# Two-layer cross-attention transformer on one core: the next phase's input loaded tile by tile in earlier steps, a fourth query group computed ahead, fewer last pairs kept off GpSimd

## The reference

```python
# layer 0
x = x + (attn(ln1(x) @ Wq, ln2(ctx) @ Wkv) @ Wproj + bproj)     # cross attention, 77 keys
x = x + (gelu(ln3(x) @ W1 + b1) @ W2 + b2)
# layer 1
h = ln1(x);  x = x + mha(h, h, sa_wq, sa_wk, sa_wv, sa_wo)      # self attention, 512 keys
h = ln2(x);  x = x + mha(h, ctx, ca_wq, ca_wk, ca_wv, ca_wo)    # cross attention, 77 keys
return x + (gelu(ln3(x) @ mlp_w1.T + b1) @ mlp_w2.T + b2)
```

## Time and profile before

| | |
|---|---|
| median of 3 runs | 3287.32 us (3286.9 to 3288.68) |
| the profiled execution | 3286.96 us, of which the traced span is 3285.1 us |
| mean granted PE clock over the span | 0.982 |
| busy in the span | PE 3139.8, PE weight loads 2496.9, DVE 1824.0, ACT 1576.0, POOL 1313.7 us |

### The profile page before, as it was taken

The page is one execution under the profiler, slowest core; times in us unless marked ns, Lnnn a source line. Parts: engine busy times, 40 slices in busy tenths (PEclk is TensorE's granted clock), DMA queues, the critical chain, the costliest instruction groups (busy, mean ns, idle before and its releaser), DMA issues.

```text
span 3285.1 us, 41887 instructions
## 1 busy us (share of the span) xinstructions
PE 3139.8 (96%) x14480; PEld 2496.9 (76%) x14480; DVE 1824.0 (56%) x2854; ACT 1576.0 (48%) x2984; POOL 1313.7 (40%) x1357
## 2 busy tenths in 40 slices
PE   6599999999999998999999999879999999999999
PEld 5478878888888876777777777557887788888887
DVE  4588884323233236887887788868888432222221
ACT  2366663322222234777776777646666332222222
POOL 0344551333333226666666666634455111111110
PEclk9799999999999999999999999989999999999999
DMA  4322223211111123344344434432222311111110
GB/s 144 113 68 89 84 75 128 68 52 52 46 44 43 41 103 107 103 124 121 99 115 123 123 97 113 119 86 67 89 83 75 118 56 39 39 39 39 39 39 13
DMA packets 215045, 264.33 MB, mean 80 GB/s; under 512 B 78459, under 2 KB 100579, under 8 KB 214835
## 3 DMA queue, kind: packets, MB, share of 16 engines
q1 hardware_dynamic: 214323, 260.87, 26.8%
q10 hardware_dynamic: 512, 0.79, 0.1%
HBM read 125.12 MB, written 60.42 MB: 56 GB/s over the span
## 4 chain that ended last, share of the span: by engine, by line
PE 82%; DVE 6%; issue 3%; SPq 2%; ACT 2%; DMA 2%; POOL 1%; ACTq 0%; DVEq 0%; POOLq 0%
PE L1sa_o L1083 5%; PE L1ff_f L110 4%; PE L1ff_f L112 4%; PE L1ff_f L111 4%; PE L1ff_acc L112 4%; PE L0ff_acc L110 4%; PE L1ff_acc L110 4%; PE L1ff_acc L111 4%; PE L0ff_f L110 4%; PE L0ff_acc L112 4%; PE L0ff_acc L111 3%; PE L0ff_f L112 3%; PE L0ff_f L111 3%; PE L1sa_pj L110 3%; PE L1sa_s L1038 3%; PE L1sa_pj L111 3%
## 5 line engine op out<-in xcount | busy, mean ns | idle before, releaser
L1216 DVE TENSOR_REDUCE L1sa_nmax<-L1sa_s 128x2 f32<-128x1024 f32 x256 | 310.5, 1213 | 130.1 <-PE L1sa_s L1038 129.1
L350 DVE TENSOR_TENSOR L1ff_gl<-L1ff_gf,L1ff_gh 128x512 fp32r<-128x512 f32 x128 | 95.4, 745 | 467.1 <-ACT L1ff_gh L336 467.1
L1308 POOL TENSOR_TENSOR L1sa_El<-L1sa_E,L1sa_Eh 128x1024 fp32r<-128x1024 f32 x122 | 299.2, 2453 | 128.5 <-ACT L1sa_Eh L1138 125.4
L350 DVE TENSOR_TENSOR L0ff_gl<-L0ff_gf,L0ff_gh 128x512 fp32r<-128x512 f32 x128 | 96.2, 752 | 414.8 <-ACT L0ff_gh L336 414.8
L324 ACT ACTIVATE L1ff_gf<-L1ff_f,cols 128x512 f32<-128x512 f32 x128 | 88.3, 690 | 450.8 <-PE L1ff_f L112 450.8
L324 ACT ACTIVATE L0ff_gf<-L0ff_f,cols 128x512 f32<-128x512 f32 x128 | 88.3, 690 | 431.6 <-PE L0ff_f L112 431.6
L1145 ACT ACTIVATE L1sa_E<-L1sa_st 128x1024 f32<-128x1024 f32 x256 | 258.7, 1011 | 6.0 <-PE L1sa_st L1050 5.9
L110 PE MATMUL L0ff_acc<-L0ff_Wh,L0ff_gh 128*128 128x512 f32 x512 | 200.2, 391 | 6.5 <-DVE L0ff_gl L350 6.5
L1138 ACT ACTIVATE L1sa_Eh<-L1sa_E 128x1024 fp32r<-128x1024 f32 x196 | 204.7, 1044 | 0.1
L110 PE MATMUL L0ff_f<-L0ca_hTh,L0ff_Wh 128*128 128x512 f32 x512 | 202.5, 396 | 0.0
L110 PE MATMUL L1ff_f<-L0ca_hTh,L1ff_Wh 128*128 128x512 f32 x512 | 202.1, 395 | 0.0
(11 more groups left out here) (313 smaller groups left out, 8507.6 us busy)
## 6 DMA issues: line engine op xcount, KB each, us to landing
L1sa_OLN<-L1sa_osb SPq DMA_DIRECT2D x128, 192.0 KB, 2.7
L1sa_stack_q<-L1sa_parts_q SPq DMA_DIRECT2D x128, 128.0 KB, 2.6
L1sa_stack_k<-L1sa_parts_k SPq DMA_DIRECT2D x124, 128.0 KB, 2.6
L0ff_xs<-x SPq DMA_DIRECT2D x60, 256.0 KB, 2.9
L1ff_xs<-x SPq DMA_DIRECT2D x60, 256.0 KB, 3.7
L0ca_stage<-in_x SPq DMA_DIRECT2D x32, 256.0 KB, 2.8
x<-L0ca_stage SPq DMA_DIRECT2D x32, 256.0 KB, 2.1
L0ff_stage<-in_L_w SPq DMA_DIRECT2D x32, 256.0 KB, 3.1
```

The source lines that it names most:

```text
L350: nc.vector.tensor_tensor(gl[:, j % 2, :], gf[:, j % 2, :], f32(gh[:, j % 2, :]), ALU.subtract)\
L1216: nc.vector.reduce_max(nmax[:, h % 2, 2 * (n % 2):2 * (n % 2) + 2], s_bank[:, :, :], AX.X, negate=True)\
L1308: nc.gpsimd.tensor_tensor(El[:, n % 2, :], E[:, n % 3, :], f32(Eh[:, n % 2, :]), ALU.subtract)\
```

## The change

1. `CA_AHEAD` is moved: the four loads of x go to steps 1, 2, 4, 7 (one each), the two raw weights to 13 and 16, statistics to 8 to 11, normalisation to 12 to 15, transposes to 17 to 20. x goes where wv's low part lay, the raw weights where wk's lay. `xs_second` is gone: batch 1 is loaded into `xs_first` once its transposes are made.
2. `first_keys` keeps only `place_k(0)`; `place_v(0)` comes after `last_residuals`, `place_k(1)` between the loads of batch 2 and the bias.
3. Query group 3 of the first batch joins `CA_FIRST`, in both cross attentions; its evacuation comes at s = 5.
4. `LAST_PAIRS` is 8: pairs 244 to 247 (steps 20 to 23) follow the usual pattern, with Eh of 245 and 247 and El of 244 and 246 on POOL.
5. The last head is copied into a buffer of its own, `osb_last`, and does not wait for the DMA of the head before.

```diff
-    osb = ph.sb("osb", [3 * HD, S])
+    osb, osb_last = (ph.sb(n, [3 * HD, S]) for n in ("osb", "osb_last"))
...
-                    if b == B - 1 and s == CA_AHEAD.load:
-                        ca.first_loads(sp)
+                    if b == B - 1 and s in CA_AHEAD.load:
+                        ca.first_load(sp, CA_AHEAD.load.index(s))
+                    if b == B - 1 and s in CA_AHEAD.raw:
+                        ca.first_weights(sp, CA_AHEAD.raw.index(s))
...
-                if h > 0:
+                if h == HEADS - 1:
+                    act.wait_ge(ca.x.e_hl.sem, ca.x.e_hl.at(0, KT - 1))
+                elif h > 0:
                     act.wait_ge(e_oln.sem, e_oln.no(h - 1))
...
-CA_FIRST = [("Q", 0, g) for g in range(3)]
+CA_FIRST = [("Q", 0, g) for g in range(G)]
...
-CA_AHEAD.load, CA_AHEAD.stats, CA_AHEAD.norms = 10, (12, 13, 14, 15), (17, 18, 19, 20)
-CA_AHEAD.transposes, CA_AHEAD.weights = (21, 22, 23, 24), (26, 27)
+CA_AHEAD.load, CA_AHEAD.stats, CA_AHEAD.norms = (1, 2, 4, 7), (8, 9, 10, 11), (12, 13, 14, 15)
+CA_AHEAD.raw, CA_AHEAD.weights, CA_AHEAD.transposes = (13, 16), (26, 27), (17, 18, 19, 20)
...
-LAST_PAIRS = 12
+LAST_PAIRS = 8
...
     def second_loads(sp):
-        sp.wait_ge(wt.lo.sem, wt.lo.no(WQ - 1))
+        sp.wait_ge(x.e_tr.sem, x.e_tr.at(0, KT - 1))
...
         place_k(sp, 0)
-        place_v(sp, 0)
-        place_k(sp, 1)
...
                 second_loads(sp)
                 sa.last_residuals(sp)
+                place_v(sp, 0)
...
                 load(sp, 2, t)
+            place_k(sp, 1)
             sp.dma_start(x.bias[:, :], bo_row.partition_broadcast(P)).then_inc(x.bias_in.sem, x.bias_in.unit)
...
                 if s == 1:
-                    for u in CA_FIRST[2:]:
-                        evacuate(*u)
+                    evacuate(*CA_FIRST[2])
...
+                if s == LEAD - 1:
+                    evacuate(*CA_FIRST[3])
```

More of the change, by code:

```diff
@@ L939, in line_up @@
                 sp.dma_start(OLN[HD * (h % 4):HD * (h % 4 + 1), :, :],
-                             osb[:, :]).then_inc(e_oln.sem, e_oln.unit)
+                             (osb_last if h == HEADS - 1 else osb)[:, :]).then_inc(e_oln.sem, e_oln.unit)
             ff.emitted(sp, B - 2)
@@ L1148, in o_out @@
                 act.wait_ge(e_pv.sem, e_pv.no(2 * h + 1))
-                if h > 0:
+                if h == HEADS - 1:
+                    act.wait_ge(ca.x.e_hl.sem, ca.x.e_hl.at(0, KT - 1))
+                elif h > 0:
                     act.wait_ge(e_oln.sem, e_oln.no(h - 1))
-                nc.scalar.activation(osb[:, :], o_bank[h % 2][0:KD, :], ACT.Copy).then_inc(e_ob.sem, e_ob.unit)
+                nc.scalar.activation((osb_last if h == HEADS - 1 else osb)[:, :], o_bank[h % 2][0:KD, :], ACT.Copy)\
+                    .then_inc(e_ob.sem, e_ob.unit)
             def m_copy(h):
@@ L1632 @@
             "wkl": 73728, "wvl": 81920, "wol": 90112, "parts_q": 98304, "parts_k": 102400, "V": 106496, "Eh": 122880,
-            "E": 131072, "El": 143360, "osb": 151552, "hs": 153600, "hTh": 157696, "oTh": 165888, "hTl": 174080,
-            "oTl": 182272, "rx": 190464, "OLN": 194560, "Vst": 200704, "rx_last": 200704, "onorm": 208384,
-            "nmax": 210432, "mm": 210464, "mT": 210528, "bqs": 211040, **{f"raw{i}": 65536 + 4096 * i for i in range(8)}}
+            "E": 131072, "El": 143360, "osb": 151552, "hs": 153600, "osb_last": 153600,
+            "hTh": 157696, "oTh": 165888, "hTl": 174080, "oTl": 182272, "rx": 190464, "OLN": 194560, "Vst": 200704,
+            "rx_last": 200704, "onorm": 208384, "nmax": 210432, "mm": 210464, "mT": 210528, "bqs": 211040, **{f"raw{i}": 65536 + 4096 * i for i in range(8)}}
 FF_OVER_OUTPUT = 4
@@ L1712, in cross_attention, with taken @@
     units = list(CA_FIRST)
+    def taken(kind, b, i):
+        return exists(b) and (kind, b, i) not in CA_FIRST
     for b in range(B):
         for kind, ahead, i in CA_ORDER:
-            if exists(b + ahead):
+            if taken(kind, b + ahead, i):
                 units.append((kind, b + ahead, i))
@@ L1754, in x_of @@
     def x_of(n):
-        return (xs_first, xs_second, x.xs)[min(n, 2)]
+        return xs_first if n < 2 else x.xs
     def load(sp, n, t):
@@ L1896, in lo, with first_load, first_weights @@
         ln_lo(nc, x, c).then_inc(x.e_hl.sem, x.e_hl.unit)
-    def first_loads(sp):
+    def first_load(sp, t):
+        if sa is not None and t == 0:
+            sp.wait_ge(sa.e_unit.sem, sa.values_done)
+        load(sp, 0, t)
+    def first_weights(sp, i):
         if sa is not None:
             sp.wait_ge(sa.e_unit.sem, sa.keys_done)
-        for t in range(TT):
-            load(sp, 0, t)
-        load_weights(sp, wt, 0, WQ)
+        load_weights(sp, wt, i, i + 1)
     def second_loads(sp):
-        sp.wait_ge(wt.lo.sem, wt.lo.no(WQ - 1))
+        sp.wait_ge(x.e_tr.sem, x.e_tr.at(0, KT - 1))
         for t in range(TT):
@@ L1967, in _ @@
             if sa is None:
-                first_loads(sp)
+                for t in range(TT):
+                    first_load(sp, t)
+                for i in range(WQ):
+                    first_weights(sp, i)
                 first_keys(sp)
+                place_v(sp, 0)
                 load_weights(sp, wt, WQ, WO)
@@ L2235, in _ @@
                 if s == 1:
-                    for u in CA_FIRST[2:]:
-                        finish(*u)
+                    finish(*CA_FIRST[2])
                 if s == 1 and sa is not None:
@@ L2338, in cross_attention @@
     ca.x, ca.hT, ca.TILES = x, hT, TILES
-    ca.first_loads, ca.first_keys, ca.zeros, ca.statistics, ca.rsqrt = first_loads, first_keys, zeros, statistics, rsqrt
+    ca.first_load, ca.first_weights, ca.first_keys = first_load, first_weights, first_keys
+    ca.zeros, ca.statistics, ca.rsqrt = zeros, statistics, rsqrt
     ca.normalise, ca.T, ca.whole, ca.hi, ca.lo = normalise, T, whole, hi, lo
```

9 lines of the change are left out of this document (6 added, 3 removed).

## The result

The changed kernel takes 3276.34 us (median of 7 runs, 3273.92 to 3278.64), the kernel before 3287.32 (median of 7 beside it, 3285.47 to 3289.64): ratio 0.9967, 95% interval 0.9955 to 0.9978, so 11.0 us or 0.33% faster. The profiled execution took 3278.37 us, span 3276.5. Forecast was 3273, range 3264 to 3282: the time is 3 us above the forecast and inside its range. Which terms hold is read by stage. Profiled executions of kernels that are the same up to there reach the last batch some 4 us apart (s9 is at 2073.2 us here and at 2077.3 in e1_last12), so durations between two marks are used, not ends. A mark "s16" is the start of PV's low matmul of step 16 of the last batch.

What follows compares the result with a forecast made beforehand. PE was taken as the bound, in flight 3139.8 of 3285.1 us. The terms, 3.5 + 6.3 + 0.5 + 3.9 = 14.2 us, off the profiled 3286.96 give 3272.8, at the median 3273; range 3264 to 3282.

Steps and rivals of the forecast that it cites:

- Term 1: Start of L0ca: query group 3's twelve matmuls move ahead of scores 2 into PE idle time; -3.5 us.
- The shift stays: After the start of L0ca PE is full, so the time gained there is kept.
- Term 2: PE's stall at step 14 of L1sa's last batch goes, less 0.3 remaining and 1.1 for statistics; -6.3 us.
- The loads' new places: 0: Last batch of L1sa: x loads at steps 1, 2, 4, 7 and raw weights at 13, 16 cost nothing.
- Term 3: Steps 16 to 31 of L1sa's last batch: DVE relieved, POOL becomes the bound; -0.5 us, from -6 to +7.
- in 2131.2 to 2159.7 this is won back: Later tail: pair 247's 4 to 6 us lateness is recovered, as three casts leave DVE and whole parts leave ACT.
- rival C: Tail: DVE was the whole bound and POOL keeps up; -5.9 us instead of -0.5, total 3268; chance 0.11.
- Term 4: Handover to L1ca: 4.4 from the copy, 1.3 from the clock, 1.8 lost to the later bias; -3.9 us.
- with a buffer of its own the copy follows at once: Handover: the last head's copy no longer waits for head 126's line-up DMA; gains 4.4 us.
- A: The stall moves: a load or statistic delays maxima in a PE-full step, no step-14 gain; 3279; chance 0.11.
- B: Tail: four new POOL instructions each block a DVE operation for their whole length; +6.8 us, total 3280; chance 0.13.
- D: Tail: POOL's lateness reaches the maxima; stalls of 7.7 us each, decisive from three, 3303 with four; chance 0.05.

Runs made afterwards that it cites:

- e1_last12: Changed kernel with LAST_PAIRS = 12 in place of 8, so the last twelve pairs are kept off POOL again; 3270.25 us, ratio 0.9953.
- e9_load8: Changed kernel with the fourth load of x issued at step 8 in place of step 7; 3278.77 us, ratio 0.9978.
- e10_before_last8: Kernel before the change with only LAST_PAIRS = 8 in place of 12 (item 4 alone); 3285.35 us, ratio 1.0002.
- e4_loads_step10: Changed kernel with all x and raw weight loads at step 10, statistics, normalisations, transposes at old steps, new memory places kept; 3279.46 us, ratio 0.9983.
- e5_one_osb: Changed kernel with the last head's copy, still to its own buffer, waiting again for the line-up DMA of the head before; 3276.48 us, ratio 0.9972.
- e3_three_groups: Changed kernel with only three query groups ahead, as before the change, in both cross attentions; 3279.32 us, ratio 0.9984.
- e2_bias_first: Changed kernel with the bias load issued ahead of place_k(1), as before the change; 3274.84 us, ratio 0.9969.

## Why the prediction was right, and by which steps

**Term 1 holds, with its size not sure in each execution.** -2.8 us measured for -3.5. PE's idle time at scores 3 stays (3.89 us), the group's matmuls are gone from behind it, and PE is in flight for 7.37 of those 10 us, not 9.32. "The shift stays" holds in seven of eleven executions with four groups; in the others the stage is as long as before, and the clock of that stretch is lower. I had priced the twelve matmuls at before's clock and left out that the clock itself could move.

**Term 2 holds, for a reason a little different.** The stall gave 7.6 us (16.1 to 8.5), predicted 7.7 - 0.3. s9 to s13 lost 1.2, predicted 1.1 and all of it from the statistics. In the changed kernel 0.9 of it falls at step 10, for the issue of the load of step 7; the DVE chain behind is as late by itself, as e9_load8 shows. "The loads' new places: 0" is thus wrong by up to 0.9 us, hidden by an equal one. It was costed by what stands behind `m_rows`, and not by the line-up DMA of the same step. DVE is in use for 14.43 of 14.43 us there.

**Term 3 failed in size: +4.1 for -0.5, within its bounds of -6 and +7.** Its first half came as told: DVE's list got shorter, the casts took 0.55 us each (0.6 taken), POOL became the bound. The failed step is "in 2131.2 to 2159.7 this is won back". The shift against before is -9.5 us at s16, -6.7 at s17, -1.4 at s23 and -5.4 at s31: 5.3 us lost between s17 and s23 (4 to 6 predicted), 4.0 back by s31. But these 4.0 are not the lateness won back. s23 to s31 takes 24.0 us in the changed kernel and 23.8 in e1_last12, where POOL has no splits to be late with; with the transposes at their old steps it takes 28.0 to 28.4, with 12 last pairs (before) or 8 (e10_before_last8, e4_loads_step10). So this part gains 4.0 by the work that left it, and of POOL's lateness nothing comes back. The term counted the casts that leave as what makes the lateness good, where they gain the same with or without it. Also left out was the residual load at step 17, which costs 2.8 us here and which I should have asked of SP's queue as "what is late next": before, it fell beside the stall. Without item 4 the stage is 4.9 us shorter than before (e1_last12), near rival C's 5.9, though with up to 2.5 of the oTl subtraction in it.

**Term 4 holds as a sum, by another item.** The first part is 4.4 of 4.4 us. The step "with a buffer of its own the copy follows at once" is true and idle: the gain is there without it (e5_one_osb). Of the 1.3 for the clock nothing is seen in the time to L1ff (e3_three_groups), although PE's wait for oTl fell from 4.57 to 1.84 us, the 1.9 forecast; POOL waits 8.27 us for the bias, issued behind `place_k(1)`, and 1.8 less in e2_bias_first, as put down; whether the time follows is open. The measured rest is +1.2 for +0.5, less than the 2.8 us by which this stage differs between the profiled executions of kernels that issue the bias last (379.1 to 381.9).

The terms as measured: -2.8 - 6.4 + 4.1 - 4.4 + 1.2 = -8.3, for 8.6 between the two profiled executions, and 11.0 between the medians. Of the 5.9 us by which the sum of 14.2 is missed, term 3 has 4.6. That the median comes within 3 us of the forecast is in part luck: the stages of one profiled execution leave 8.3 of the 14.2, and the start of L0ca and the oTl subtraction move an execution by some 3 and 2.5 us.

**The rivals.** A: no maxima DMA came late in steps 0 to 15; its mild form is the residual at step 17. B predicted +6.8 for the term, against +4.1; item 4 alone measured 6.5, which looks like B's 6.8, but its mechanism, a fixed price for each of POOL's four instructions, does not hold: they cost 0.9 to 1.0 with the transposes at their old steps (e4_loads_step10, e10_before_last8). Rows of the changed kernel's DVE, the first beside POOL's El of 2121.95:

```profile
2121.95 1.23 DVE L1221 TENSOR_REDUCE L1sa_nmax<-L1sa_s 128x2 f32<-128x1024 f32 x1 [0.31 <-PE L1sa_s L1040]
...
2134.54 2.21 DVE L1229 TENSOR_TENSOR L1sa_El<-L1sa_E,L1sa_Eh 128x1024 fp32r<-128x1024 f32 x1 [0.79 <-ACT L1sa_Eh L1140]
```

The maximum beside El is not stretched. The subtractions are: the one into oTl of 2102.16, shown above, by POOL's El (2101.94 to 2104.32), and this one of 2134.54 by POOL's sum of 2134.39 to 2135.66, by 1.0 us. The Trainium skill ("SBUF — State Buffer", SBUF: two separate sides) says that of a DVE operation with two inputs in on-chip memory and a POOL operation that reads there, the one that starts first has the shared port for its whole instruction and the other is fully blocked. The trace agrees for the subtractions, and e5_one_osb shows the other order: there DVE's takes 0.68 us and POOL's El 2.88 in place of 2.38. The new El of pairs 244 and 246 met mostly maxima and idle time of DVE; the collision that costs 2.5 us is with an El that was there before. C is what the stage would be without item 4. D's mechanism is there (two waits for `mm`, 1.87 and 2.38 us), far from its deciding point of three stalls of 7.7.

## What to carry to other kernels

Two edits that each load the same in-order engine in the same steps aren't costed one by one: moving the transposes with POOL's four subtractions behind them gained 4.9 us, giving POOL four splits cost 1, and both together cost 4.1. Price a share given to an engine by what stands ahead of it in that engine's list when its input is ready, and by who idles for it, since two copies of 1.03 us cost 3.1. Before a stage of one profiled execution is set against that of another, look whether the same instructions met in the same order: here 2.5 of 9.0 us were the outcome of a collision that the edit did not touch. When a stall is taken away, look through the queues for the next transfer that the stall had been covering, and when a queue is shortened and a buffer doubled for the same wait, try each alone.
